# Another order of TensorE's work inside a slot of an attention and expert kernel

## What is computed

```
zn = (z - mu) / sqrt(var + EPS) * ln_scale + ln_bias
q, k, v = heads of zn @ w_qkv
scores = einsum('bhqd,bhkd->bhqk', q, k) / SCALING
att = softmax(scores, axis=-1)
out = einsum('bhal,bhlv->bhav', att, v)
out = z + (out @ w_proj + b_proj)
```

## Time and profile before

| | us |
|---|---|
| median of three runs | 984.24 |
| profiled execution, whole | 983.9 |
| its span (first to last instruction) | 982.1 |
| TensorE matmul busy | 882.3 |
| VectorE busy | 792.7 |
| ScalarE busy | 663.7 |
| GpSimd busy | 314.5 |

### The profile page before, as it was taken

One profiled execution on the slowest core, in us unless ns is written; L12 is line 12 of the kernel. 1 busy time (PEld: TensorE's weight loads), 2 busy tenths in 40 slices (PEclk: granted clock), 3 DMA queues, 4 the chain that ended last, 5 costly groups with the idle time before them and its releaser, 6 DMA issues. The chain is left out here.

```text
span 982.1 us, 14337 instructions
## 1 busy us (share of the span) xinstructions
PE 882.3 (90%) x5188; PEld 319.8 (33%) x5188; DVE 792.7 (81%) x1568; ACT 663.7 (68%) x728; POOL 314.5 (32%) x450
## 2 busy tenths in 40 slices
PE   6879999999999999999999999999989989757985
PEld 3312322222243233322332242322322313136863
DVE  4598879898979878899888879889799788265765
ACT  5128778787877787878877868788677768901110
POOL 4041010005424414139443423255243232822113
PEclk9769999999999999999999999999999989988998
DMA  5631010310320203101411022004310001240001
GB/s 143 105 45 39 16 53 16 73 41 10 90 61 13 93 12 70 38 13 55 89 61 56 12 39 59 23 7 105 91 56 14 11 13 31 85 172 23 1 1 64
DMA packets 52375, 49.08 MB, mean 50 GB/s; under 512 B 17504, under 2 KB 43696, under 8 KB 51920
## 3 DMA queue, kind: packets, MB, share of 16 engines
q1 hardware_dynamic: 51680, 46.91, 19.4%
q0 software_dynamic: 384, 1.05, 0.3%
q10 hardware_dynamic: 240, 0.20, 0.2%
HBM read 18.06 MB, written 9.17 MB: 28 GB/s over the span
## 5 line engine op out<-in xcount | busy, mean ns | idle before, releaser
L1331 DVE TENSOR_REDUCE mx<-ring 128x1 f32<-128x512 f32 x1024 | 633.9, 680 | 110.3 <-PE ring L1038 109.6
L873 ACT ACTIVATE prob<-sc,unscale 128x1024 f32<-128x1024 f32 x512 | 539.1, 1113 | 85.2 <-PE sc L1056 83.9
L1038 PE MATMUL ring<-kp,qp 48*128 48x512 f16 x1024 | 299.4, 395 | 43.5 <-DVE mx L1331 22.5
L1070 PE MATMUL obank<-prob,vaug 128*32 128x512 f32 x2048 | 276.1, 612 | 0.7 <-ACT prob L873 0.6
L1038 PEld LDWEIGHTS ring<-kp,qp 48*128 48x128 f16 x1024 | 74.1, 93 | 361.4 <-DVE mx L1331 301.3
L1056 PE MATMUL sc<-qp,kp 64*128 64x512 f16 x1024 | 167.9, 381 | 14.0 <-ACT prob L873 13.3
L644 POOL TENSOR_TENSOR parts<-qkf,parts 128x1024 f16<-128x1024 f32 x14 | 29.9, 2134 | 209.6 <-ACT parts L803 209.6
L1056 PEld LDWEIGHTS sc<-qp,kp 64*128 64x128 f16 x1024 | 50.4, 95 | 92.3 <-ACT prob L873 83.9
L631 POOL TENSOR_TENSOR hid<-hid,b 128x512 f32<-128x512 f32 x24 | 30.2, 1270 | 110.9 <-ACT hid L827 110.9
L639 POOL TENSOR_TENSOR yA<-yA,sums 128x512 f32<-128x512 f32 x15 | 19.0, 1269 | 131.1 <-DMA sums<-reciprocal_scratch 131.1
L1070 PEld LDWEIGHTS obank<-prob,vaug 128*32 128x32 f32 x2048 | 40.5, 108 | 61.5 <-issue 58.4
(11 more groups left out here) (221 smaller groups left out, 749.2 us busy)
## 6 DMA issues: line engine op xcount, KB each, us to landing
x_sb<-x SPq DMA_DIRECT2D x7, 1024.0 KB, 6.0
kp<-parts SPq DMA_DIRECT2D x48, 128.0 KB, 4.4
qp<-parts SPq DMA_DIRECT2D x93, 64.0 KB, 5.5
out<-hid SPq DMA_DIRECT2D x4, 1024.0 KB, 5.3
yA<-oT SPq DMA_DIRECT2D x124, 32.0 KB
sums<-reciprocal_scratch SPq DMA_DIRECT2D x31, 128.0 KB
x_scratch<-x SPq DMA_DIRECT2D x3, 1024.0 KB, 4.5
qp<-mp SPq DMA_DIRECT2D x128, 2.0 KB
```

The lines of the kernel that those rows point to most:

```text
L873: nc.scalar.activation(prob[:, e % 2, 2 * a:2 * a + 2, :].rearrange("p g n -> p (g n)"), sbuf2[a][:, :], ACT.Exp, scale=unscale[:, 0:1]).t ...
L1038: nc.tensor.matmul(dst[:, :], qp[rows, qh, h, qt * P:(qt + 1) * P], kp[rows, h, kh * HALF:(kh + 1) * HALF], start=True, stop=True).then_in ...
L1070: ins = nc.tensor.matmul(obank[i * VW:(i + 1) * VW, :], vaug[:, b % 2, kt, c0:c0 + VW], prob[:, v % 2, i, :], start=(kt == 0), stop=(kt == ...
L1331: nc.vector.tensor_reduce(mx[:, u % 2, n:n + 1], src[:, :], AX.X, ALU.max).then_inc(rv_free, 1)
```

## The change

TensorE's order in a slot from 12 on becomes: m0, m1, value product of two slots ago (it was one), m2, m3, items, scores. The number of slots grows by one, since the last value product falls a slot later. VectorE does the four reductions first, then mt, then its side work. ScalarE copies the output bank one slot later, ahead of items and exponentials; the DMAs and reciprocals that follow from it, and GpSimd's multiplications, move by one slot.

```diff
-SLOTS = NS + LEAD + 3
+SLOTS = NS + LEAD + 4
-D_AT = (43, 51, 14, 19)
+D_AT = (44, 52, 15, 20)
...
-        at[t] = mt + fill + pairs[0] + pairs[1] if e >= 0 else pairs[0] + mt + fill + pairs[1]
+        at[t] = pairs[0] + pairs[1] + mt + fill if e >= 0 else pairs[0] + mt + fill + pairs[1]
...
-                    first = 8 * u + 8 + LEAD + (4 if u % HU == 0 else 1)
+                    first = 8 * u + 9 + LEAD + (4 if u % HU == 0 else 1)
...
+                if e % 8 == 1 and 8 < e <= NS + 1:
+                    u = e // 8 - 1
+                    sc.wait_ge(s_av, 8 * u + 8)
...
-                if e % 8 == 0 and 0 < e <= NS:
...
-                if e >= 0:
-                    items()
                 if t < NS:
                     max_products(range(0, 2))
-                if 0 <= e < NS:
-                    scores(0)
-                    scores(1)
                 if e < 0:
                     items()
...
+                if 0 <= e - 2 < NS:
+                    value_product(e - 2)
                 if t < NS:
                     max_products(range(2, 4))
-                if 0 <= e - 1 < NS:
-                    value_product(e - 1)
+                if e >= 0:
+                    items()
+                if 0 <= e < NS:
+                    scores(0)
+                    scores(1)
...
-                    if key[0] == "mt" or e < 0 and key[0] == "max" and key[2] < 2:
+                    if key[0] == "mt" or key[0] == "max" and (e >= 0 or key[2] < 2):
                         ring_item(key)
...
-                    if t == 8 * u + 8 + LEAD + (6 if u % HU == 0 else 3):
+                    if t == 8 * u + 9 + LEAD + (6 if u % HU == 0 else 3):
                         reciprocals(u)
...
-                    if key[0] == "max" and (e >= 0 or key[2] >= 2):
+                    if e < 0 and key[0] == "max" and key[2] >= 2:
```

More of the change, by code:

```diff
@@ L859, in _ @@
                 e = t - LEAD
+                if e % 8 == 1 and 8 < e <= NS + 1:
+                    u = e // 8 - 1
+                    sc.wait_ge(s_av, 8 * u + 8)
+                    if u >= NH:
+                        sc.wait_ge(s_rows[u % NH], ROWS * (u // NH))
+                    nc.scalar.activation(oT[:, u % 2, :], obank[:, :], ACT.Copy).then_inc(s_oT, 1)
                 for key in RING_AT[t]:
@@ L874, in _ @@
                                              sbuf2[a][:, :], ACT.Exp, scale=unscale[:, 0:1]).then_inc(s_free, 1)
-                if e % 8 == 0 and 0 < e <= NS:
-                    u = e // 8 - 1
-                    sc.wait_ge(s_av, 8 * u + 8)
-                    if u >= NH:
-                        sc.wait_ge(s_rows[u % NH], ROWS * (u // NH))
-                    nc.scalar.activation(oT[:, u % 2, :], obank[:, :], ACT.Copy).then_inc(s_oT, 1)
                 if 1 <= w < B and tau in (46, 48):
@@ L1434, in _ @@
                 for u in range(B * HU - 1):
-                    if t == 8 * u + 8 + LEAD + (6 if u % HU == 0 else 3):
+                    if t == 8 * u + 9 + LEAD + (6 if u % HU == 0 else 3):
                         reciprocals(u)
-                if t == SLOTS - 5:
+                if t == SLOTS - 6:
                     ve.wait_ge(s_rows[1], ROWS * (B * HU // NH - 1))
```

## The result

The changed kernel took 1004.91 us (median of four runs, 1004.44 to 1005.54) against 984.33 for the kernel before, measured beside it: 1.0208 times, 95% interval 1.019 to 1.0226. The forecast was 1005.6. The profiled execution has a span of 1002.8 us against 982.1, so 20.7 us are to be found in the trace.

The account below looks back on a forecast made before the run. A 2.49 us loop through TensorE and VectorE, no engine's own work, was taken as the bound. Item slots +20.8 and the rest +0.9 made +21.7 on 982.1, 1003.8; with 1.8 outside the span 1005.6, own range 998 to 1009.

Parts of the forecast that it names:

- "v", queries and keys: Slots with these items and those behind: +3.6 "v" with transpose, +3.0 queries and keys alone, +7.1 with transpose.
- "z", "u", "x": Item slots and those behind: short transposes "z", "u" +6.2 with the transpose of the maxima, "z" alone +0.5; "x" pairs +1.8.
- the head: Exponentials trail the maxima by half a slot more and set the pace behind the last maxima: +1.2.
- "p", "h", "w": 18 item slots without a transpose, each with the slot behind: -0.08 each, -1.4 in all.
- the output bank: ScalarE's evacuation of the output bank falls behind queries and "h", where exponentials are late already: 6 x 0.2, +1.2.
- Plain slots, 2.49: Slots without items: the same four-piece loop through TensorE and VectorE stays 2.49, nothing gained.
- The third bank and the transpose: Item slots: first item waits for a max product's bank, 1.80 instead of 1.63; 2.49 with the transpose in front.
- Late exponentials: Behind items, scores wait for exponentials ahead of the next maxima: tail 4.84, 5.48 after queries and keys, against 4.67 unhindered.
- Statistics in the last window, -2.5: Last window's slots without items: value product runs beside VectorE's statistics, giving back 1.2 and 1.3.
- a rival for late results: Reciprocals made later hold up GpSimd's division and so TensorE at "p", up to 2 per window: 1008 to 1012, chance 0.20.
- VectorE's side work at no cost: VectorE's side work behind the maxima costs the same as ahead of them.
- the fast rival: Item slots: overlap comes through, banks free and no exponential late, about -19, so 965; chance 0.05.

Follow-up runs that it names:

- 8: Version with long items first, short ones and transpose between the max pairs, value product two slots behind, now cut into 384 and 128 columns: 1004.9 us, 1.0183.
- 5: Kernel after, with the transpose of the maxima behind the items; VectorE does maxima, side work, then the transpose's two operations: 993.8 us, 1.0087.
- 4: Kernel after, with ScalarE's second copy of queries and keys cut from 512 to 32 columns in windows 2 to 4: 997.9 us, 1.0133.
- 11: Kernel after, with both the reordering of 5 and the short copy of 4: 990.4 us, 1.0067.
- experiment 10: Kernel before, with the second copy of queries and keys cut from 512 to 32 columns in windows 2 to 4: 982.6 us, 0.9973.
- 9: Kernel before; in 30 long-item slots TensorE does m0, m1, scores, items, m2, m3, value product, VectorE's side work between second and third reductions: 974.1 us, 0.989.
- 12: As 9, but the transpose of the maxima stands between the two items, its two VectorE operations behind the side work: 973.3 us, 0.9892.
- 3: Kernel before, with only VectorE's side work moved behind the four maxima, TensorE's order unchanged: 1023.2 us, 1.04.
- 6: Kernel after, with VectorE's side work put back ahead of the maxima, the transpose's operations behind them: 1079.2 us, 1.0952.

## Why the prediction was right, and where it was not

The large terms came in by their mechanism: "v", queries and keys, "z", "u", "x" and the transposes in plain slots were forecast at 23.2 us together and measured 22.4. That the total is off by 1 us only is in part luck. Among the rest, +1.2 for the head and +2.3 for the late reciprocals were missing, and -2.1 for "p", "h", "w", -1.2 for the output bank and -0.6 for the tail stood against them.

- **Plain slots, 2.49.** Right, and the reason too: with the value product split (8) they fall to 2.36 to 2.39. The loop through both engines set them.
- **The third bank and the transpose.** Right (5). The reduction that frees the bank starts too late for an item in that place.
- **Late exponentials.** Right in size (4, 11: 0.40 for 0.40) and in place; they cost ScalarE nothing, TensorE's scores wait for them with the next maxima behind.
- **"p", "h", "w".** The term was 2 us off. The tail of 4.84 behind the items measured 4.73 (293.40 less 290.10 is 3.30, where 4.84 less 1.43 is 3.41), and for "w" I had taken the projections' difference, where the pair went from 6.90 to 6.7.
- **Output bank behind queries, +1.2.** Wrong: 0. The step said that the copy would fall where the exponentials are late already. The slots behind queries are 3.30 with the copy (5) and without it (36).
- **Statistics in the last window, -2.5.** The number came out and the reason did not. I said that the value product now runs beside the statistics. But experiment 10, which has the order before, has the same gain at the first place:

```profile
713.04 0.39 PE L1039 MATMUL ring<-kp,qp 48*128 48x512 f16 x1 [1.51 <-DVE mx L1332]
713.36 1.06 PE L1071 MATMUL obank<-prob,vaug 128*32 128x512 f32 x8
```

  The stall of the earlier trace rows is there, 1.51, and the two slots behind it take 4.99 in place of 6.13. What differs is the granted clock, the third figure from the end of these rows; kernel before, then experiment 10:

```profile
714.00:717.00 3.00, 3.00 (x20) 0.70 (x16) 3.00 (x6) 1.93 (x2) 2.81 (x4) 0.52 0.03 3
```

```profile
714.00:717.00 3.00, 2.85 (x22) 0.67 (x20) 3.00 (x7) 1.93 (x2) 2.72 (x5) 1.00 0.03 3
```

  The order gave nothing that can be seen: at full clock slots 25 to 28 took 11.66 after and 11.67 with the order before (9, 10, 12), and slots 33 to 36 took 12.87 in both. The last place likewise: experiment 9 has the order before there and took 10.7 for three slots at full clock, where the earlier trace rows have 13.3. The term should have been 0, with 1.2 at the first place and 2.3 at the last for the clock (the two slots behind the stall, 7.3 in the kernel before and 5.0 in experiment 9); that it came out at -2.4 is luck.
- **What was not in it: late reciprocals in the last window, +2.3.** I had a rival for late results, but at "p" and through GpSimd. TensorE did not wait at "p". It was the reciprocals of slot 17, and their DMA, issued a slot later behind four DMAs of keys; they came 7.4 us behind its issue. In the kernel before it stood behind two of them (673.57), and the reciprocals followed 3.7 us later without a wait:

```profile
695.78 0.61 SPq L411 DMA_DIRECT2D total<-oT  x1
...
703.22 0.25 DVE L1316 RECIPROCAL over<-total 128x16 f32<-128x16 f32 x1 [1.00 <-DMA total<-oT]
...
704.08 0.39 PE L1038 MATMUL ring<-kp,qp 48*128 48x512 f16 x1 [0.69 <-DVE mx L1331]
```

  The clock then stood at 0.50 from 705 to 708. Of the 2.3, 0.7 to 1.0 is the wait; that the rest is the clock is read from that row, no run took it apart.
- **VectorE's side work at no cost.** Right for the change as a whole, and I did not say on what it hangs. VectorE's half alone costs 39 us (3), TensorE's without it 74 more than both together (6).
- **The head.** Half a slot of phase was in the sum with 1.2; measured 2.4. Kernels with the head's order before start their first value product anywhere from 74.0 to 75.5, so over 1 us of it need not be the order's. The granted clock rises between 75.8 and 78 there, behind that value product; what moves it stays open.

The rule of the Trainium skill ("Perfetto Trace Analysis", section "Identifying the Most-Contended Engine") that I weighed says to optimize the engine with the highest occupancy first. I read it as: feed VectorE, and so it spoke for the fast rival. For this change the trace went against it. But experiment 9 does feed VectorE during the items, and gains 8 us by it: 0.41 of the 3.65 us of idleness in a slot, no more.

## What to carry to other kernels

Price a new order by the loop of waits in it, with who frees each buffer, and not by the overlap that a picture promises; a buffer is free from its reader's start plus the reader's latency, here 0.74 us. In-order queues must be moved together: work that is hidden is hidden beside something, and when that moves on one engine, the hidden work has to move on the others. And compare a term with a second kernel before believing its reason: a number that came out can be the clock's.

## What the runs showed of the hardware

- The granted clock of TensorE did not follow from the stall alone. With TensorE standing 1.51 us for the same row and the same order around it, it went to half (0.52) in one kernel and stayed at 1.00 in another. That spell cost 1.2 us. Spells at the other places with statistics, in kernels with the same order there, cost from 0.1 (13.00 for 12.87, experiment 10, slots 33 to 36) to 2.3 us (7.29 for 4.98, kernel before against experiment 9, slots 50 and 51).
- Behind a stall of 4.2 us it was at the low level, 0.50 from 414 to 419 and 0.55 in 419 to 421, and two projections took 6.33 us for 3.7 (experiment 6).
- Kernels with the same head differed by up to 1.4 us in when their slots began, which moves the whole; differences of 1 us between kernels are to be read slot by slot.
- A value product cut into 384 and 128 columns took 0.78 and 0.36 to the next instruction, together 1.14 in place of 1.00.
